# A scan on pairs of channel halves, filler matmuls around it, and earlier expert loads, in a Macaron block on one NeuronCore

## The reference, cut to what matters

```python
dt = softplus(dt_r @ dt_proj_w.T + dt_proj_b)
dA = exp(dt[..., None] * A)                      # 256 channels, 16 states
dBx = dt[..., None] * Bv[:, :, None, :] * xc[..., None]
h = dA_t * h + dBx_t                             # over 512 tokens, h0 = 0
y = einsum('bdn,bn->bd', h, C_t)                 # sum over the 16 states
out = (y + xc * D) * silu(z) @ out_proj_w.T
```

## Time and profile before

| | |
|---|---|
| runs | 1758.99, 1762.87, 1764.25 us |
| profiled execution | 1760.58 us, of which the span from first to last instruction is 1758.8 us |
| mean granted TensorE clock | 0.974 of 2.4 GHz |
| F1 | to 159 us |
| mixer: projections / softplus / scan | 159 to 212 / 212 to 224 / 224 to 478 us |
| F2 | 478 to 642 us |
| E1A, attention, E1B, attention | from 642, 862, 997, 1214 us |
| E2A, E2B | from 1349, 1560 us |

### The profile page before, as it was taken

How to read it: one execution, slowest core, us unless ns; L and a number is a source line. 1 busy time by engine, 2 the same in 40 slices (tenths; PEclk the granted TensorE clock), 3 DMA queues, 4 the chain that set the end, 5 groups by cost and what they waited for, 6 DMA issues and landing times.

```text
span 1758.8 us, 24391 instructions
## 1 busy us (share of the span) xinstructions
PE 1605.8 (91%) x6936; PEld 1196.0 (68%) x6936; DVE 1272.3 (72%) x2156; ACT 1016.4 (58%) x2065; POOL 992.7 (56%) x955
## 2 busy tenths in 40 slices
PE   7997667877799989999899899998998999999998
PEld 5775323333367767777688677886886778878887
DVE  5555699999855756788578567885775678856665
ACT  4343655454434446676477666664776666656665
POOL 1101067766510028888433378894333888978887
PEclk9999789999999999999999999999999999999999
DMA  2000000000000036666300056663000566656674
GB/s 104 10 1 1 0 1 1 0 0 0 8 0 1 1 88 165 163 166 165 85 1 1 6 143 154 170 174 86 1 1 5 146 152 174 172 141 172 172 173 107
DMA packets 57678, 136.75 MB, mean 78 GB/s; under 512 B 10251, under 2 KB 33251, under 8 KB 57187
## 3 DMA queue, kind: packets, MB, share of 16 engines
q1 hardware_dynamic: 57571, 135.47, 30.0%
HBM read 133.33 MB, written 2.10 MB: 77 GB/s over the span
## 4 chain that ended last, share of the span: by engine, by line
PE 64%; DVE 4%; ACT 3%; issue 2%; POOL 2%; POOLq 0%; PEldq 0%; PEld 0%; DMA 0%; SPq 0%; DVEq 0%; ACTq 0%
PE ps L226 18%; PE ps L227 18%; PE ps L228 17%; PE ps L1488 2%; PE ps L1473 1%; PE ps L1474 1%; PE ps L1475 1%; PE ps L774 1%; POOL m_hc L984 1%; POOL e_lo L234 1%; PE ps L366 1%; PE ps L1476 0%; DVE p L1661 0%; PE ps L377 0%; PE ps L254 0%
## 5 line engine op out<-in xcount | busy, mean ns | idle before, releaser
L234 POOL TENSOR_TENSOR e_lo<-e_h,e_hi 128x512 fp32r<-128x512 f32 (+1 forms) x368 | 476.4, 1295 | 131.1 <-ACT e_hi L231 120.7
L1140 ACT ACTIVATE e_s<-ps 128x512 f32<-128x512 f32 (+1 forms) x368 | 220.4, 599 | 271.5 <-PE ps L228 270.8
L1296 DVE TENSOR_TENSOR ps<-e_s,ps 128x512 f32<-128x512 f32 x352 | 244.7, 695 | 179.3 <-PE ps L228 145.1
L226 PE MATMUL ps<-xn_hi,eh 128*128 128x512 f32 x704 | 284.8, 405 | 10.3 <-ACT e_s L1140 7.4
L227 PE MATMUL ps<-xn_lo,eh 128*128 128x512 f32 x704 | 279.5, 397 | 0.0
L228 PE MATMUL ps<-xn_hi,el 128*128 128x512 f32 x704 | 278.8, 396 | 0.0
L1301 DVE TENSOR_TENSOR e_h<-ps,rwb 128x512 f32<-128x512 f32 x352 | 243.3, 691 | 16.2 <-DVE ps L1296 4.8
L984 POOL TENSOR_TENSOR m_hc<-m_h,m_c 128x512 f32<-128x512 f32 x128 | 172.5, 1348 | 125.3 <-DVE m_h L940 122.9
L234 POOL TENSOR_TENSOR el<-e_raw,eh 128x128 fp32r<-128x128 f32 (+1 forms) x352 | 221.8, 630 | 26.7 <-ACT eh L1129 26.7
L231 ACT ACTIVATE e_hi<-e_h 128x512 fp32r<-128x512 f32 (+1 forms) x368 | 229.3, 623 | 7.4 <-DVE e_h L1301 7.3
L774 PE MATMUL ps<-m_hc,const 128*128 128x512 f32 x256 | 149.5, 667 | 48.8 <-POOL m_hc L984 43.9
(11 more groups left out here) (232 smaller groups left out, 3293.5 us busy)
## 6 DMA issues: line engine op xcount, KB each, us to landing
e_raw<-in_experts SPq DMA_DIRECT2D x176, 192.0 KB, 3.9
rwb<-rw_rows SPq DMA_DIRECT2D x64, 352.0 KB
rwb<-rw_rows SPq DMA_DIRECT2D x80, 256.0 KB
rwb<-rw_rows SPq DMA_DIRECT2D x32, 320.0 KB
rwb<-rw_rows SPq DMA_DIRECT2D x48, 192.0 KB
rwb<-rw_rows SPq DMA_DIRECT2D x32, 224.0 KB
rwb<-rw_rows SPq DMA_DIRECT2D x32, 160.0 KB
rwb<-rw_rows SPq DMA_DIRECT2D x80, 64.0 KB
```

The lines of the kernel that those rows point to most:

```text
L226: pe.matmul(out, w_hi, x_hi, start=start, stop=False, skip_group_check=True)
L234: return eng.tensor_tensor(lo, full, hi.bitcast(F32), ALU.subtract)
L1140: act.activation(e_s[0:rows_, buf, :], ps[0:rows_, 4, :], ACT.Silu).then_inc(S["silu"], 1)
L1296: dve.tensor_tensor(ps[:, bank, :], e_s[:, buf, :], ps[:, 5, :], ALU.mult).then_inc(S["gated"], 1)
```

## The change

- The scan works on states n alone (16 a block), both halves in one instruction of 1024 elements: the input term writes two banks (`terms(n)`, banks 0 and 1, or 6 and 7) from one spread of B in bank 3 read with step 0 over the halves; the scan runs over 1024 elements in a line, and a zero at the first element of the second half of `m_da` (set once by GpSimd) restarts it; GpSimd's product is 1024 elements. There are two buffers of pairs in place of four of items.
- The input term of n + 1 now waits for the scan of n - 1, which is the instruction ahead of it on VectorE. TensorE spreads B one pair later than before, when the last input term is done, and adds up both halves of n - 1 after that.
- `softplus_end` and `dt_times_xc` of a block follow one another directly after items 0, 1 and 2 of block 0.
- The output projection writes bank 2, where C is spread too. So C of item 4 of the next block (HEAD = 5) is spread only after the residual's addition, which VectorE does after the scan of item 4; ScalarE copies it ahead of the exponentials of item 5. Items 0 to 4 carry `finish`: `ylin` after item 1 when both halves are summed, `gated` and g_hi after item 2 (before: `gated` after the third item and g_hi after the fourth, of half the size), g_lo and the output projection after item 3, the addition after item 4.
- `spin` is added in the mixer: 20 after the last layer norm, 8 before each `in_proj` in the loop, 18 before the last `x_proj` and 8 after it, 12 before the last output projection, 6 at the mixer's end; and at both attentions' ends 10 before the last output projection and 6 behind it.
- SyncE issues the first four expert loads when F2 starts, and the store of the routing rows behind them.

```diff
-        ITEMS, HEAD = DS * MC, 8
-        DEEP = 4
-        B_BANKS, C_BANK, SPREAD_AHEAD = (0, 1, 3, 7), 2, 3
+        HEAD = 5
+        DB_BANKS, B_BANK, C_BANK = (0, 6), 3, 2
+        def both(tile, n):
+            return tile[:, MC * (n % 2):MC * (n % 2) + MC, :]
+        def in_line(v):
+            return v.rearrange("p m t -> p (m t)")
+        def terms(n):
+            first_bank = DB_BANKS[n % 2]
+            return ps[:, first_bank:first_bank + MC, :]
...
@@ mix_pe
+            spin(pe, 6, 20)
             pe.wait_ge(*M("dt_w", 2))
             pe.wait_ge(*L("xn_lo", NB))
             with pe.Fori(0, NB - 1) as i:
+                spin(pe, 6, 8)
                 in_proj(i + 1, bass.ds((i + 1) * T, T))
                 x_proj(i)
+            spin(pe, 6, 18)
             x_proj(NB - 1)
+            spin(pe, 6, 8)
...
+            def spread_b(i, blk, n):
+                after(pe, "db", DS * i + n)
+                pe.matmul(ps[:, B_BANK, :], sel_bc[:, n, :], bc[:, blk], start=True, stop=True).then_inc(M["b_spread"], 1)
...
+            def item(i, blk, n, last):
+                if n + 2 < DS:
+                    spread_b(i, blk, n + 2)
+                elif not last:
+                    spread_b(i + 1, following, n + 2 - DS)
+                if n == HEAD - 1:
+                    after(pe, "x_new", i)
+                    spread_c(i, blk, n)
+                if n + 1 < DS and n + 1 != HEAD - 1:
+                    spread_c(i, blk, n + 1)
+                elif n + 1 == DS and not last:
+                    spread_c(i + 1, following, 0)
+                if n:
+                    total(i, n - 1)
+                elif not (isinstance(i, int) and i == 0):
+                    total(i - 1, DS - 1)
...
@@ mix_act
+            def item(i, blk, n, last):
+                after(act, "h", DS * i + n - 1)
+                for m in range(MC):
+                    act.activation(both(m_da, n)[:, m, m:T], dt_b[:, m, m:T], ACT.Exp,
+                                   scale=neg_a[:, m * DS + n:m * DS + n + 1]).then_inc(M["da"], 1)
+                act.wait_ge(*M("c_spread", DS * i + n + 1))
+                after(act, "hc", DS * i + n - 1)
+                act.activation(m_c[:, n % 2, :], ps[:, C_BANK, :], ACT.Identity).then_inc(M["c_copy"], 1)
...
@@ mix_dve
+            def input_term(i, blk, n):
+                dve.wait_ge(*M("b_spread", DS * i + n + 1))
+                after(dve, "h", DS * i + n - 1)
+                dve.tensor_tensor(terms(n), du[:, :, blk], of_both(ps[:, B_BANK, :]), ALU.mult).then_inc(M["db"], 1)
...
+                dve.tensor_tensor_scan(in_line(both(m_h, n)), in_line(both(m_da, n)), in_line(terms(n)), 0.0,
                                        ALU.mult, ALU.add).then_inc(M["h"], 1)
+                if isinstance(i, int) and i == 0 and n + 1 < NB:
+                    softplus_end(n + 1)
+                    dt_times_xc(n + 1)
...
@@ mix_pool
+                pool.tensor_tensor(both(m_hc, n), both(m_h, n), of_both(m_c[:, n % 2, :]), ALU.mult).then_inc(M["hc"], 1)
...
@@ heads in att_pe, last block
+                else:
+                    spin(pe, 0, 10)
                 out_proj(i, HEADS - 1)
+                if last:
+                    spin(pe, 0, 6)
...
@@ moe_load_first, and SyncE's program
+            if not before:
+                moe_store_rows(sp, R, half)
...
-            moe_store_rows(sp, R1, 0)
             moe_load_first(sp, E1A, 0, R1, None)
...
             mix_pe(pe, LN[1])
+            spin(pe, 0, 6)
             end_phase(pe)
```

More of the change, by code:

```diff
@@ L205, in program @@
             "bc_hi bc_lo v nabs e ln dt du b_spread c_spread da db h c_copy hc y_sum ylin "
-            "gated g_hi g_lo out x_new aexp bc_zero dt_b").split(), 0), 1)
+            "gated g_hi g_lo out x_new aexp bc_zero dt_b da_zero").split(), 0), 1)
         A, = group("att", dict.fromkeys((
@@ new lines, in total, with finish @@
+            def total(i, n):
+                pe.wait_ge(*M("hc", DS * i + n + 1))
+                for m in range(MC):
+                    if n == 0:
+                        after(pe, "ylin", 2 * i + m - 1)
+                    last = pe.matmul(ps[:, 4 + m, :], ident, both(m_hc, n)[:, m, :], start=(n == 0), stop=(n == DS - 1),
+                                     skip_group_check=True)
+                last.then_inc(M["y_sum"], 1)
+            def finish(i, blk, n):
+                if n == 0 and isinstance(i, int):
+                    total(i, DS - 1)
+                if n == 3:
+                    if isinstance(i, int):
+                        spin(pe, 0, 12)
+                    pe.wait_ge(*M("c_copy", DS * NB if isinstance(i, int) else DS * (i + 1) + HEAD - 1))
@@ L782, in finish @@
                         w = slice(M_OUT + m * P, M_OUT + (m + 1) * P)
-                        last = mm3(pe, ps[:, 6, :], mh[:, w], ml[:, w], g_hi[:, m, :], g_lo[:, m, :], m == 0, m == MC - 1)
+                        last = mm3(pe, ps[:, C_BANK, :], mh[:, w], ml[:, w], g_hi[:, m, :], g_lo[:, m, :], m == 0, m == MC - 1)
                     last.then_inc(M["out"], 1)
@@ L791, in mix_pe @@
             pe.wait_ge(*M("v", 2 * NB))
-            for q in range(SPREAD_AHEAD):
-                spread_b(0, cut(0), q)
+            spread_b(0, cut(0), 0)
             spread_c(0, cut(0), 0)
+            spread_b(0, cut(0), 1)
             scan_blocks(pe, item, finish)
@@ L841, in mix_act, with finish @@
             act.wait_ge(*M("aexp", 2))
-            def item(i, blk, q, last):
-                n, m = q // MC, q % MC
-                if q == 0:
+            def item(i, blk, n, last):
+                if n == 0:
                     act.wait_ge(*M("dt_b", i + 1))
[L847 to L856, removed]
+                    if isinstance(i, int) and i == 0:
+                        act.wait_ge(*M("da_zero", 1))
+                after(act, "h", DS * i + n - 1)
+                for m in range(MC):
+                    act.activation(both(m_da, n)[:, m, m:T], dt_b[:, m, m:T], ACT.Exp,
[3 more added lines that the diff above has]
+                act.activation(m_c[:, n % 2, :], ps[:, C_BANK, :], ACT.Identity).then_inc(M["c_copy"], 1)
+            def finish(i, blk, n):
+                if n == 2:
                     after(act, "out", i)
@@ L929, in item @@
+            def item(i, blk, n, last):
                 following = bass.ds((i + 1) * T, T)
-                if q == ITEMS - 2 and not last:
-                    dve.wait_ge(*M("da", 32 * i + ITEMS))
+                if n == DS - 1 and not last:
+                    dve.wait_ge(*M("da", 2 * DS * (i + 1)))
                     dt_copy(i + 1, following)
-                if q + 1 < ITEMS:
-                    input_term(i, blk, q + 1)
+                if n + 1 < DS:
+                    input_term(i, blk, n + 1)
@@ L941, in item @@
+                dve.tensor_tensor_scan(in_line(both(m_h, n)), in_line(both(m_da, n)), in_line(terms(n)), 0.0,
                                        ALU.mult, ALU.add).then_inc(M["h"], 1)
[L943 to L948, removed]
+                if isinstance(i, int) and i == 0 and n + 1 < NB:
+                    softplus_end(n + 1)
+                    dt_times_xc(n + 1)
+                    if n + 2 == NB:
```

85 lines of the change are left out of this document (30 added, 55 removed).

## The result

The changed kernel took 1777.5 us (median of 4 runs, 1774.6 to 1778.5) against 1762.5 before (4 runs): ratio 1.0085, 95% interval 1.0065 to 1.0105. It is slower by 15 us (0.85%, clear of the runs' scatter) where 5.7 were forecast, 8.9 us above the forecast time and 0.5 us above the range. The profiled execution took 1774.6 us, span 1772.7.

A forecast was written before the change was run, and what follows sets the result against it. TensorE was busy 91% of the span, but VectorE was taken to bound the scan. Scan +22.1 less savings 16.4 gave net +5.7 on 1760.6, 1766.3; with 2.3 added, 1768.6 us, range 1753.5 to 1777.

The forecast's parts named there:

- With the same order now: 2.4 + 6.7 + 6.7: Scan's three block turns: VectorE gets the port first once, GpSimd twice; 15.8 against 5.4 before, +10.4 us.
- rival 1: GpSimd first at every turn of the scan: +14.7 for +10.4, 1772.9 us; chance 0.15.
- TensorE [...] may run at half clock behind it: +1: Scan's turns: TensorE waits some 2 us several times and may then run at half clock; +1 us (0 to 3).
- So 0.12 comes back: 3.43 a pair, 60 pairs +0.6 us: Middle of the scan: the term's wait for the scan ahead returns 0.12 a pair; +0.6 us (−6 to +4).
- (a): Port collision at back-to-back `softplus_end` and `dt_times_xc`: GpSimd's product gets in, three times 2.2 us, +6.6 (0 to 6.6).
- Start +0.8: Scan's start: first scan needs both exponentials, second input term a later spread; +0.8 us (0.6 to 1.5).
- End +2.7: Scan's end: longer last product, a second fp32 matmul and a second `ylin`; +2.7 us (2 to 3.5).
- F2 −4.3: F2's layer norm: its matmuls run at full clock instead of 1.2 GHz; −4.3 us (−1 to −4.5).
- Attention's ends −2.6: Both attentions' ends: −1.8 at the first, −0.8 at the second, where the clock fell later; −2.6 us (+0.8 to −3).
- Rival 2: VectorE keeps the port over back-to-back instructions, softplus pair too: scan 6.9, net −9.5, 1753.4 us; chance 0.18.
- rival 3: The handover from scan to input term is free: −6 for +0.6, net −0.9, 1762 us; chance 0.14.
- rival 4: The spins don't hold the clock, only E1A's 5.4 remains: net +16.7, 1779.6 us; chance 0.08.

The follow-up runs named there:

- the wait alone: Kernel before, with each input term also waiting for the scan just ahead of it on VectorE: 1785.9 us, ratio 1.0124.
- C shifted: Changed kernel, output projection taking the C bank one item later, so C of item 5, not 4, waits for the addition: 1770.1 us.

## Why the prediction missed

The forecast had the sign right, and the kinds of loss that it named were all there. What failed is the sum of the scan, +22.1 where the runs show +29.4. Three steps were too small there: the order at the first turn (by 4.3), TensorE at half clock in the turns (by 2.2) and the handover (by 1.8); the smaller terms and a remainder of 0.6 take 1.0 back. The savings came out 2.0 lower. None of these by itself leaves the range; together they did.

**"With the same order now: 2.4 + 6.7 + 6.7": wrong, 4.3.** The step gave VectorE the port at the turn from 0 to 1. GpSimd had it at all three. The order of the trace before was no property of the scan's loop: in the kernel before with spins and loads, and in the one with the wait alone, the same two instructions took 2.34 there and not 1.27, with the same lead of 0.3 us. So rival 1 was the case, and at its price: a turn's 3.0 for `gated` and item 3 came as 3.42 for 1.27 and a wait of 0.78, 2.9. The rule cited from the Trainium skill (SBUF — State Buffer, Who interferes with whom) gave all three turns to GpSimd, and here the trace agrees (3.41, 3.42, 3.42); at the one turn it still doesn't.

**"TensorE [...] may run at half clock behind it: +1": too small, by 2.2.** VectorE's term of item 7 waited 1.01, 1.01 and 1.19 for its spread of B, 3.2 us in all. I had followed the late C to ScalarE and not to what is queued behind it on TensorE: the spread of C of item 5, the sum of a pair, then the spread of B. All of them ran at 0.50 or 0.57 granted. From the rows at either clock (3.62 for 1.98 in the sum alone) I estimate that at full clock the spread would have come 1.6 us sooner, and the wait of 1.0 with it would be gone. No run held the clock there, so this share is an estimate; that the late C starts the wait is shown by the run with C shifted, which has neither the wait at item 5 nor the one at item 7. The 1.5 for item 5 came as 1.77, 1.77, 1.30.

**"So 0.12 comes back: 3.43 a pair, 60 pairs +0.6 us": too small, by 1.8.** The step took the handover from L915 and its dependent, 0.03 after its end. Behind the scan it is 0.10 to 0.11, in the changed kernel and in the kernel before with the wait alone, where nothing else differs. A pair in the middle costs 0.10 more than an old one. In the trace 44 terms follow a scan directly, +4.4. At 18 terms another instruction stands between the scan and the term and covers the gap (three softplus pairs; at each turn `dt_copy`, `ylin`, `gated`, g_lo and the addition), and there the joining's 0.11 is kept, −2.0. That leaves +2.4, inside the step's bounds. A row of another kind of instruction was not the nearest price: the trace of before had no dependent scan.

**The rest of the scan.** (a) `softplus_end` and `dt_times_xc`, +6.6: right, 3.25 for 1.20, three times, 6.2 by the rows and 5.9 by the time of the kernel with them apart. g_lo 2.2: measured 2.16. Start +0.8: about +1.3 (block 0, from the first term to the first `dt_copy`, grew by 8.3; less 6.2 for (a) and 1.1 for 11 gaps, and 0.3 more for the three terms without one). End +2.7: +2.2 (from the last scan's end to the last addition to x, 7.7 and 9.9).

The rows of the three turns (`gated`, g_lo and the waits at items 3, 5 and 7) add up to 23.3, less 5.4 before: +17.9, where 10.4 and 1 were forecast. A check on that: from one `dt_copy` to the next the two middle blocks grew by 7.86 and 5.65 us, and these rows with 11 gaps and five spared ones in each give 7.88 and 5.68. All together it is 2.4 + 1.3 + 6.2 + 17.9 + 2.2 = 30.0 for the 29.4 measured.

**Savings 16.4: 14.4.** Projections −4.1: measured −4.1. E1A −5.4: −5.36, and by loads alone the same. F2 −4.3: −3.6 to the first normalising, of which 3.1 were left at `f_s`. That these 3.1 were left is luck of the profiled executions: 23.0 us before against 20.6 to 20.7 in three other kernels without the end spins, 19.9 after against 23.1 in three others with them. Attention's ends −2.6: −1.8 is what is left of the whole; from E1B's first matmul to its third shared product it is 5.11 for 6.7.

**The rivals.** Rival 1 was right about the order and too low by the other steps. Rival 2 is out by GpSimd's order at all three turns, rival 3 by the gap of 0.11, rival 4 by the savings.

## What to carry to other kernels

Before you join two instructions into one of double length, ask whether the number of buffers stays. Here it fell to two, so the producer had to wait for the consumer just ahead on the same engine; each wait cost 0.21 us, twice what the joining saved (0.11 a pair). Pairs without that wait weren't tried. Where two engines share a port, don't put two instructions that need it back to back: a scan between them took 6 us off the time here, and one instruction for two took 14 off the three turns (9.6 off the time). Follow a late instruction down every queue that it stands in, and price what is behind it at the granted clock that the rows show behind such waits. Try each part of a change by itself: the spins and loads gave 13 us, and the pairs, which cost 28 beside them, hid it; with these collisions and waits mended the pairs came level with single halves in the scan, no better. And add up what happens when several terms go wrong the same way before you set a range.

## What the runs showed of the hardware

- A VectorE instruction that waits for the one just ahead of it mostly started 0.10 to 0.11 us after a scan's end (both lengths of scan), but 0.03 after an elementwise product of 1024. In the changed kernel 3 of 44 terms came 0.03 to 0.04 after their scan, one behind the last scan of each of the first three blocks. Why they differ stays open.
- Who gets the port in a collision is not settled by a lead of 0.3 us: with 0.31 and 0.30 between the same two instructions at the first turn, VectorE's second half went first in the kernel before (and in it with early loads), GpSimd's product in the kernel before with spins and loads (and in it without the end spins, and with the wait alone), one profiled execution each. With pairs the lead is 0.16, and GpSimd's product went first at all 15 turns of the five profiled kernels that kept `gated` in halves.
- A GpSimd product that had to wait for a VectorE instruction of 1.20 us took 3.25 where it takes 2.36: the loss goes the other way, and was hidden here.
- TensorE's granted clock does not come back, or stay, the same way each time. In F2's layer norm, entered at 0.50 with the same 3.78 us for the first four records, the first normalising came after 10.8 us in the kernel before and after 8.5 in the one without the spins at the scan's end. Entered at 1.00, with the same 7.2 us to the first normalising, it fell to 0.50 some 12 us after the last addition to x in three kernels and stayed at 1.00 in three.
